# Attention on one Trainium2 core: the clamp of the row maxima is dropped, and a bound on the last key's exponential moves into the sum

## The reference, cut to what matters

```python
q_r = jnp.einsum('bshq,hqr->bhsr', q_big, W_qr)
k_r = jnp.einsum('bld,hdr->bhlr', kv_rope, W_kr)
scores = jnp.einsum('bhsr,bhlr->bhsl', q_r, k_r)
attn = jax.nn.softmax(scores, axis=-1)
ctx_c = jnp.einsum('bhsl,bld->bhsd', attn, kv_rope)
```

## Time and profile before

| | |
|---|---|
| median of 3 executions | 1015.87 us (1010.46 to 3312.19) |
| profiled execution: its own time | 1010.17 us |
| profiled execution: span | 1008.3 us |
| TensorE busy | 956.7 us, 95% of the span |
| VectorE busy | 554.6 us, 55% |
| ScalarE busy | 412.2 us, 41% |
| GpSimd busy | 453.6 us, 45% |

### The profile page before, as it was taken

One profiled execution on the slowest core, in us unless ns is written; L12 is line 12 of the kernel. 1 busy time (PEld: TensorE's weight loads), 2 busy tenths in 40 slices (PEclk: granted clock), 3 DMA queues, 4 the chain that ended last, 5 costly groups with the idle time before them and its releaser, 6 DMA issues. The chain is left out here.

```text
span 1008.3 us, 16001 instructions
## 1 busy us (share of the span) xinstructions
PE 956.7 (95%) x5497; PEld 805.8 (80%) x5497; DVE 554.6 (55%) x1039; ACT 412.2 (41%) x956; POOL 453.6 (45%) x490
## 2 busy tenths in 40 slices
PE   6999977999899988999999999989999999999997
PEld 5677756888777867888888988767778899999997
DVE  5433479888899935444545233327967333333345
ACT  2434457777777724233332043453433122222111
POOL 2898845555666520000000302127705878992051
PEclk9999989999999999999999999999999999999999
DMA  8688713111111105222230014320024857571152
GB/s 250 211 269 261 213 34 95 43 43 38 37 32 33 54 1 184 87 84 84 85 102 21 11 42 153 111 71 30 1 87 129 273 167 246 192 227 53 43 166 96
DMA packets 79004, 109.93 MB, mean 109 GB/s; under 512 B 14224, under 2 KB 46992, under 8 KB 78928
## 3 DMA queue, kind: packets, MB, share of 16 engines
q1 hardware_dynamic: 66288, 82.18, 26.5%
q10 hardware_dynamic: 10080, 18.35, 5.2%
q0 software_dynamic: 2560, 8.39, 2.5%
HBM read 83.13 MB, written 25.77 MB: 108 GB/s over the span
## 5 line engine op out<-in xcount | busy, mean ns | idle before, releaser
L43 PE MATMUL psum<-second_xT_hi,second_w_hi 128*128 128x512 f32 x272 | 107.3, 395 | 3.8 <-PEq L74 2.9
L44 PE MATMUL psum<-second_xT_lo,second_w_hi 128*128 128x512 f32 x272 | 106.7, 392 | 0.0
L45 PE MATMUL psum<-second_xT_hi,second_w_lo 128*128 128x512 f32 x272 | 106.6, 392 | 0.0
L1242 POOL TENSOR_TENSOR all_x<-all_x,mlp_raw 128x512 f32<-128x512 f32 x8 | 10.0, 1295 | 174.7 <-DVE all_x L1744 174.7
L2262 ACT ACTIVATE moe_s<-psum 128x352 f32<-128x352 f32 x39 | 18.2, 466 | 151.0 <-PE psum L45 151.0
L2328 DVE TENSOR_TENSOR moe_hT_lo<-psum,moe_hT_hi 128x384 fp32r<-128x384 f32 x39 | 21.8, 558 | 78.8 <-ACT moe_hT_hi L2268 78.8
L43 PEld LDWEIGHTS psum<-second_xT_hi,second_w_hi 128*128 128x128 f32 x272 | 51.5, 189 | 16.4 <-issue 3.5
L1699 ACT ACTIVATE mlp_s<-psum,mlp_side 128x512 f32<-128x512 f32 x32 | 21.9, 683 | 100.2 <-PE psum L45 100.2
L43 PE MATMUL psum<-moe_w_hi,moe_tT_hi 128*128 x184 | 61.3, 333 | 0.0
L1744 DVE TENSOR_TENSOR all_x<-all_x,psum 128x512 f32<-128x512 f32 x64 | 43.8, 687 | 31.7 <-PE psum L45 31.2
L45 PEld LDWEIGHTS psum<-second_xT_hi,second_w_lo 128*128 128x128 f32 x272 | 51.5, 189 | 10.9
(11 more groups left out here) (346 smaller groups left out, 2892.4 us busy)
## 6 DMA issues: line engine op xcount, KB each, us to landing
kv_all<-all_x ACTq DMA_DIRECT2D x28, 256.0 KB, 5.3
far_raw<-in_eg SPq DMA_DIRECT2D x10, 704.0 KB, 4.6
far_raw<-in_eu SPq DMA_DIRECT2D x10, 704.0 KB, 4.2
slot_rows<-mix_W SPq DMA_DIRECT2D x23, 256.0 KB, 5.8
slot_out<-far_rows ACTq DMA_DIRECT2D x23, 256.0 KB, 2.3
far_raw<-in_ed SPq DMA_DIRECT2D x10, 512.0 KB, 4.2
far_rows<-slot_rows ACTq DMA_DIRECT2D x19, 256.0 KB, 2.8
second_raw<-in_w_feat SPq DMA_DIRECT2D x18, 256.0 KB, 3.4
```

The lines of the kernel that those rows point to most:

```text
L43: e.matmul(out, hi_l, hi_r, start=first, stop=False)
L44: e.matmul(out, hi_l, lo_r, start=False, stop=False)
L45: return e.matmul(out, lo_l, hi_r, start=False, stop=last)
L1242: pool.tensor_tensor(g["x"][:, t, :], g["x"][:, t, :], b2, ALU.add).then_inc(x_plus, 1)
```

## The change

The tile `zero`, its memset on GpSimd and the minimum with it (L1009, 64 instructions) go, with the semaphores `top_ok` and `zero_set`. `low` is now the negated maximum itself, which may be positive when all 256 scores are negative; then the last key's exponential can be large, up to infinity. The sum of L1015 becomes one scalar_tensor_tensor that takes the minimum of that exponential and 2^126, and adds the total. The number of instructions there stays the same: 64.

```diff
-        zero = n.sb("zero", [P, 2])
...
+        MOST = 2.0 ** 126
...
             pool.wait_ge(heads.rot, B)
-            pool.memset(zero[:], 0.0).then_inc(zero_set, 1)
             pool.memset(g["power"][:], -0.5).then_inc(power_set, 1)
...
                 wait(v, exp_ok, NJ * (b - 2) + 2 * i + 2)
-                v.tensor_reduce(pair(low, b, i), scores_of(b, i), AX_X, ALU.max, negate=True).then_inc(top_ok, 1)
-                v.wait_ge(top_ok, 2 * b + i + 1)
-                v.tensor_tensor(pair(low, b, i), pair(low, b, i), zero[:], ALU.min).then_inc(low_ok, 1)
+                v.tensor_reduce(pair(low, b, i), scores_of(b, i), AX_X, ALU.max, negate=True).then_inc(low_ok, 1)
...
                 v.wait_ge(last_ok, done)
-                v.tensor_tensor(pair(scale, b, i), pair(total, b, i), pair(last, b, i), ALU.add).then_inc(sum_ok, 1)
+                v.scalar_tensor_tensor(pair(scale, b, i), pair(last, b, i), MOST, pair(total, b, i), ALU.min, ALU.add).then_inc(sum_ok, 1)
...
             v.wait_ge(heads.kept, 1)
-            v.wait_ge(zero_set, 1)
```

More of the change, by code:

```diff
@@ L758, in attention_programs @@
         q_hi_ok, q_ok = S_("q_hi_ok"), S_("q_ok")
-        sc_ready, top_ok, low_ok, exp_ok, last_ok, sum_ok, inv_ok, pr_ok = (S_(x) for x in (
-            "sc_ready", "top_ok", "low_ok", "exp_ok", "last_ok", "sum_ok", "inv_ok", "pr_ok"))
+        sc_ready, low_ok, exp_ok, last_ok, sum_ok, inv_ok, pr_ok = (S_(x) for x in (
+            "sc_ready", "low_ok", "exp_ok", "last_ok", "sum_ok", "inv_ok", "pr_ok"))
         pt_ready, pt_hi_ok, pt_ok = (S_(x) for x in ("pt_ready", "pt_hi_ok", "pt_ok"))
@@ L763, in attention_programs @@
         pr_far_ok = S_("pr_far_ok")
-        stats_ok, wb_in, power_set, zero_set = S_("stats_ok"), S_("wb_in"), S_("power_set"), S_("zero_set")
+        stats_ok, wb_in, power_set = S_("stats_ok"), S_("wb_in"), S_("power_set")
         up_in, up_hi_ok, up_ok = S_("up_in"), S_("up_hi_ok"), S_("up_ok")
```

## The result

Over 20 executions of each kernel the changed one took 1011.74 us in the median (1005.53 to 1024.06), the kernel before 1017.29 (1010.46 to 3312.19). The ratio is 0.9951, with a 95% interval of 0.9930 to 0.9972: faster by 5.0 us, 2.8 to 7.1. The ratio leaves out executions in a slower state of the chip, such as the one of 3312 us, while the medians take in all 20, and so differ by 5.6. By the bound of 2% that is no difference; by its own interval it is one. The prediction's gain of 4.9 us came out almost to the digit. Its time of 1005.3 us did not: the median lies 6.4 above it. As a step from the median of 1017.29, 1005.3 would be a gain of 12 us.

What follows compares the result with a forecast made beforehand. The prediction took TensorE, busy 95% of the span, as the bound. Terms of 1.7 + 2.0 + 1.2 = 4.9 us, taken from the profiled 1010.17 us, gave 1005.3 us, with a range of 1000 to 1013.5 us.

Steps and rivals of the forecast that it cites:

- the last term of the sum: The base that the 4.9 us gain was taken from: the profiled execution's 1010.17 us, giving 1005.3 us.
- The bound by idle TensorE: Attention: the edit pays only where TensorE idles, at most 20.2 us; nothing from 178 to 257 us.
- The minimum is held to the end of GpSimd's instruction: Attention's minima: one starting while GpSimd reads SBUF ends with GpSimd's instruction; two thirds of 30.2 us are waiting.
- No surcharge for the new sum: Sum in each attention step: the scalar_tensor_tensor costs what the plain sum did, so zero was added.
- The rival of a dearer sum: Attention's sums: the new form costs up to 0.24 us more, 8 us in all; chance 0.1.
- Steps 0 to 5: Start of the attention: 0.2 in step 0, 0.5 each in steps 2 to 4, otherwise 0; 1.7 us.
- Steps 18 to 28: Attention steps with GpSimd's longer batch: sums slip through earlier, scaled copies end earlier; 2.0 us saved.
- Step 31: Last attention step: without the held first minimum ScalarE starts earlier, cutting TensorE's 1.40 us idle; 1.2 us saved.
- What would show it: Signs in the changed profile: TensorE idle near 10 and 5 us in the outer stretches, new sum's mean about 0.3 us.
- the hold passes on: Attention: the next pair of SBUF inputs inherits all held time; gain only 1.8 us, 1008.4 us; chance 0.2.
- The full return: All 17 steps bound by VectorE lose two minima and their gaps; 17.3 us gained, 992.8 us; chance 0.1.
- A slower kernel: Steps 19 to 28: VectorE's full product wins over GpSimd's next instruction, so GpSimd pays; 1014.2 us; chance 0.1.

Runs made afterwards that it cites:

- e1: The kernel before, run again with no edit as a second profile; ratio to the kernel before 1.0007.
- e2: The changed kernel, run again with no edit as a second profile; ratio to the kernel before 0.9955.
- e7: The kernel before with GpSimd's three subtractions for low parts replaced by memsets to zero; 198.53 us from step 0 to step 31.
- e10: The kernel before with each 128x2 clamp made as two one-column minima with an immediate; ratio 0.9955.
- e3: The kernel before with the clamp as a minimum with an immediate, one SBUF input, instead of a tile of zeros; ratio 1.0005.
- e4: The kernel before with the clamp kept and the plain sum replaced by the new scalar_tensor_tensor; ratio 1.0011.
- e5: The changed kernel without the bound: no clamp, and the plain addition as the sum; ratio 0.9956.
- e11: The changed kernel with the bounded sum made column by column, two 128x1 tensor_scalar instead of one scalar_tensor_tensor; ratio 0.9994.
- e6: The kernel before with the clamp made twice, one minimum behind the other; 227.63 us from step 0 to step 31.
- e9: The changed kernel with two more waits on GpSimd, ahead of L211 and L233; ratio to the kernel before 0.9954.
- e12: The changed kernel with both the two GpSimd waits and the sum by column; ratio to the kernel before 0.9951.
- e13: The changed kernel with the two GpSimd waits, and the sum by column only in steps 19 to 28; ratio to the kernel before 0.9910.

## Why the prediction was right or wrong

**What failed** is the last term of the sum: "against the profiled execution's 1010.17 us". The working took one execution for the kernel's time. It named the median of 1015.87, 5.7 above, and set it aside because the lowest agreed with the profile; both were low. With 20 executions the kernel before has 1017.29 in the median, 7.1 above the profile, and counted from there 4.9 us give 1012.4, beside the measured 1011.74. In the later runs, on three chips, the same kernel had medians of 1012.0 to 1012.8, so the base moved by 5 us, about what the change is worth. The runs show where most of that scatter is (e1, e2): ahead of the attention's first reduction and behind its last, not in the steps that the sum is about. The range held the time, through the allowance at its upper end.

**The size** was right, in part by luck: 0.8 to 1.0 us of clock in steps 0 to 5, which no term had, and 0.7 more in steps 18 to 30 stand against a step 2 that gave nothing and a step 31 that gave half. The terms:

- *The bound by idle TensorE* held. Steps 6 to 17 took 78.99 us before and 79.08 after, with VectorE 7 us less busy.
- *The minimum is held to the end of GpSimd's instruction*: shown. In the kernel before, 49 of the 64 minima took over 170 ns, and 48 of them ended 0.01 to 0.02 us behind the end of a GpSimd instruction that reads SBUF. In e7 those beside a memset were not held. That the gain is mostly the hold's is shown by e10, where 2.2 of the 2.7 us of steps 18 to 30 come back with the clamp left in. The condition was stated too narrowly, as two SBUF inputs; e3 was held with one.
- *No surcharge for the new sum*: shown by e4 and e5. The rival of a dearer sum is out: 236 and 219 ns against 236 and 220.
- *Steps 0 to 5*, 1.7 us: 2.3 to 2.5. Step 0 gave the 0.2 and step 1 its 0. Step 3 gave 0.5, though not quite as worked out. There the exponentials begin 0.37 us after the reduction's end, as they did after the minimum's (155.10 against 154.73), and not the 0.10 assumed; the sum comes 0.27 later than in the working, and L840 ends just then, so that nothing is held and nothing lost. Step 4 gave 0.6, and there the new sum is held to the end of L840, as worked out. Here is that step in the changed kernel, ScalarE's and GpSimd's rows too:

```profile
162.89 1.28 POOL L840 TENSOR_TENSOR first_xT_hi<-queries_q,first_xT_hi 128x512 fp32r<-128x512 f32 x1
...
163.68 0.51 DVE L1013 SCALAR_TENSOR_TENSOR att_scale<-att_last,att_total 128x2 f32<-128x2 f32 x1 [0.72 <-ACT att_last L961]
164.12 0.47 ACT L959 ACTIVATE att_pr<-psum,att_low 128x256 f32<-128x256 f32 x1
164.22 0.17 DVE L1015 RECIPROCAL att_scale<-att_scale 128x2 f32<-128x2 f32 x1
164.42 0.69 DVE L1019 TENSOR_TENSOR att_pr<-att_pr,att_scale 128x512 f32<-128x512 f32 x1
```

  Step 2, counted at 0.5, gave 0.05. The clock was low at the end of step 1 and the start of step 2 (0.72 between 146 and 152 us, above), so that the second reduction waits 0.28 us for the scores:

```profile
151.22 0.69 DVE L1007 TENSOR_REDUCE att_low<-psum 128x2 f32<-128x512 f32 x1 [0.28 <-PE psum L45]
```

  The trace of before had a low clock there too, 0.78 between 146 and 152 us; the working had read only the one of step 5. Step 5, put at 0, gave 1.0 against the first profile, where its clock was low, and 0.2 against e1, where it wasn't. The steps that the clock didn't lengthen gave 0.2, 0.5, 0.6 and 0.2, in steps 0, 3, 4 and 5: 1.5 us.
- *Steps 18 to 28*, 2.0 us: 2.5 (step 18 0.2, step 21 0.4, 22 0.2, 23 0.4, 25 0.4, 26 0.2, 27 and 28 0.4 each; 19, 20 and 24 nothing), and steps 29 and 30 together another 0.2. The pattern is that of the working. Steps 21, 23, 25, 27 and 28, worked out at 0.3 us each, gave 0.4. In step 21 the sum slips out at L840's end and L211 holds the product; in step 22 the hold of L233 passes to L204. VectorE in the changed kernel:

```profile
276.48 0.53 DVE L1013 SCALAR_TENSOR_TENSOR att_scale<-att_last,att_total 128x2 f32<-128x2 f32 x1 [0.71 <-ACT att_last L961]
277.05 0.17 DVE L1015 RECIPROCAL att_scale<-att_scale 128x2 f32<-128x2 f32 x1
277.25 1.54 DVE L1019 TENSOR_TENSOR queries_q<-queries_q,att_scale 128x512 f32<-128x512 f32 x1
...
284.17 1.50 DVE L204 TENSOR_SCALAR queries_q<-all_x,att_mv,att_rstd 128x512 f32<-128x512 f32 x1 [0.28 <-POOL att_rstd L196]
```

  and GpSimd:

```profile
276.96 1.28 POOL L211 TENSOR_TENSOR all_x<-all_x,queries_q 128x512 f32<-128x512 f32 x1
...
284.11 1.27 POOL L233 TENSOR_TENSOR second_xT_lo<-queries_q,second_xT_hi 128x512 fp32r<-128x512 f32 x1
```

- *Step 31*, 1.2 us: 0.7. TensorE's 1.40 us before the context fell to 0.72, because VectorE then waits for ScalarE's high part. On VectorE and TensorE of the changed kernel:

```profile
350.22 1.29 DVE L1024 TENSOR_TENSOR first_xT_lo<-psum,first_xT_lo 128x512 fp32r<-128x512 f32 x2 [0.52 <-ACT first_xT_lo L968]
```

```profile
351.61 0.47 PE L43 MATMUL psum<-first_xT_lo,first_xT_hi 128*128 128x512 f32 x1 [0.72 <-issue]
```

  The term took TensorE's wait to be VectorE's alone. By the steps the whole gain is 4.9 to 5.0 us up to step 31 and 0.7 behind it, 5.6 to 5.7, inside the interval of 2.8 to 7.1 and 0.7 to 0.8 above the 4.9 forecast, about what the clock gave.
- *What would show it*: TensorE's idle in the outer two stretches was to fall to 10 and 5 us; it is 11.1 and 6.3, but the stretches lie elsewhere in the steps here, as said. Laid at the steps' own edges, idle fell from 10.7 to 9.8 us in steps 0 to 5 (the four lines with the clocks, above) and from 6.9 to 5.6 in 18 to 30, by 0.9 and 1.3 where 1.7 and 2.0 were forecast. In steps 0 to 5 the rest is TensorE's busy time, 23.7 against 22.2 us at the higher clock; in 18 to 30 it is busy time too, 89.2 against 87.8, without a change of clock, which stays open. The mean of the new sum was to be about 0.3 us or more; it is 0.219, since only 12 of the 64 are held; before the others GpSimd's batch is over or all but over, as in step 3. L840, L196 and L211 did not start later: in steps 19 to 28 they begin within 0.02 us of their place before, counted from the step's first reduction.

The rivals: the hold passes on in steps 1, 20 to 28 (products, L204), but not everywhere, and 1.8 us is too little. The full return, 17.3 us, is too much; VectorE waits for ScalarE instead, 22.0 us ahead of the sums. A slower kernel did not show, and GpSimd's unmoved starts speak against its mechanism.

## What to carry to other kernels

A tiny VectorE instruction on SBUF can cost three times its length beside GpSimd: compare its shortest with its median, and its end with GpSimd's ends, before counting it. Giving it a shape that isn't held (one column here) can be worth more than half of removing it, and two of them in a row can cost the kernel far more than twice what one does. Look at the granted clock of each stretch before a difference between two profiles is put down to the change. And when executions scatter by 1%, count a gain of 0.5% from the median of many, and judge it by the steps it touches.

## What the runs showed that I had not expected

- A one-input minimum of 128x2 in SBUF is held beside GpSimd (median 559 ns in e3), one of 128x1 never (142 to 157 ns in e10). A two-input one is held by GpSimd's subtractions but by none of its memsets (160 to 164 ns in e7).
- A 128x1 tensor_scalar of two operations with a pointer scalar takes 205 ns (e11); with immediates alone it takes 149 ns with one operation (e10) and 144 with two (L191 in the changed kernel).
- Between two GpSimd instructions back to back, a VectorE instruction that is already waiting gets through, but one that began 0.09 us after GpSimd's next waits for all of it (e6: 1.20 us).
- Doubling the minimum cost 18 us where removing it gave 5. Half of it is in steps 6 to 17, where VectorE's time had been hidden: TensorE idles 4.8 us there in e6, and 0.2 in the kernel before.
- In steps 0 to 5 the mean granted clock was 0.95 in five profiles without the clamp (the changed kernel's three, e5, e9) and 0.85 to 0.90 in four with it (before, e1, e3, e4); but e11, e12 and e13, without it too, had 0.85 to 0.90. What sets it is open.
